# A recommender tower on one core: one first load, one batch of transposes in another PSUM bank, filler matmuls, every row gather held behind TensorE, and a small GpSimd write behind each gather of the last two tiles

## The reference, cut to what matters

```
e = stack([tbl_f[ids[:, f]] for f in range(26)], axis=1)      # 512 x 26 x 128
sd = einsum('bfd,bd->bf', e, dense)
ss = einsum('bfd,bgd->bfg', e, e);  pairs = ss[:, iu, ju]     # triu, k=1
z = concatenate([dense, sd, pairs], axis=1)
h = concatenate([z, dense], axis=1)                            # 607 columns
h = maximum(h @ W_top1 + b_top1, 0)                            # 512
h = maximum(h @ W_top2 + b_top2, 0)                            # 256
y = h @ W_top3                                                 # 1
```

## Time and profile before

| | us |
|---|---|
| median of 3 runs | 152.84 |
| the profiled execution's own time | 151.2 |
| its span, first to last instruction | 149.4 |
| TensorE busy | 108.6 |
| VectorE busy | 79.9 |
| ScalarE busy | 66.7 |
| GpSimd busy | 66.0 |

### The profile page before, as it was taken

One profiled execution on the slowest core, in us unless ns is written; L12 is line 12 of the kernel. 1 busy time (PEld: TensorE's weight loads), 2 busy tenths in 40 slices (PEclk: granted clock), 3 DMA queues, 4 the chain that ended last, 5 costly groups with the idle time before them and its releaser, 6 DMA issues.

```text
span 149.4 us, 2760 instructions
## 1 busy us (share of the span) xinstructions
PE 108.6 (73%) x1074; PEld 95.6 (64%) x1074; DVE 79.9 (53%) x217; ACT 66.7 (45%) x151; POOL 66.0 (44%) x66
## 2 busy tenths in 40 slices
PE   7799961999999925500001957958997999799794
PEld 7588831888888805400001947948986998699782
DVE  5699919979999274000750020680386189248401
ACT  4463309737786053000502041693398288145620
POOL 7787747768787778777783752000000000000000
PEclk9999996599999996855555699996999999999999
DMA  4877961576999422111120211000000000000000
GB/s 116 257 193 188 247 191 36 175 183 199 305 287 249 153 53 53 53 53 53 35 52 19 57 35 42 2 0 4 4 0 0 4 0 0 4 4 0 0 0 1
DMA packets 5030, 12.35 MB, mean 83 GB/s; under 512 B 1725, under 2 KB 1853, under 8 KB 5018
## 3 DMA queue, kind: packets, MB, share of 16 engines
q1 hardware_dynamic: 3002, 8.09, 18.8%
q0 software_dynamic: 1920, 3.94, 10.3%
q10 hardware_dynamic: 96, 0.15, 0.4%
HBM read 12.18 MB, written 0.00 MB: 82 GB/s over the span
## 4 chain that ended last, share of the span: by engine, by line
PE 47%; issue 16%; DVE 14%; another core or an unknown queue 13%; ACT 9%; ACTq 0%
PE dots L443 19%; DVE pairs L347 12%; PE dots L487 12%; PE hidden L512 4%; PE hidden L542 3%; PE turned L467 3%; ACT embT L310 2%; ACT high L299 2%; PE dots L421 2%; ACT embT L285 2%; ACT pairs L285 2%; PE turned L512 1%; DVE embT L347 1%; PE last_layers L535 1%
## 5 line engine op out<-in xcount | busy, mean ns | idle before, releaser
L249 POOL DMA_INDIRECT rows<-tbl,gather_idx x60 | 63.3, 1055 | 24.2 <-issue 16.5
L354 DVE TENSOR_SCALAR onehot<-ids_h 125x512 fp32r<-125x512 f16 x88 | 33.4, 435 | 22.5 <-issue 13.9
L443 PE MATMUL dots<-onehot,high 125*128 125x512 f32 (+1 forms) x88 | 36.0, 426 | 0.0
L347 DVE COPY pairs<-dots 27x128 f32<-27x128 f32 (+8 forms) x88 | 23.7, 270 | 21.7 <-PE dots L487 19.1
L467 PE MATMUL turned<-ident,rows 128*128 128x128 f32 x60 | 10.8, 305 | 31.7 <-ACT embT L285 21.5
L443 PE MATMUL dots<-onehot,low 125*128 125x512 f32 (+1 forms) x88 | 32.9, 389 | 0.3 <-issue 0.3
L467 PEld LDWEIGHTS turned<-ident,rows 128*128 128x128 f32 x60 | 7.6, 154 | 34.8 <-issue 34.1
L285 ACT COPY pairs<-dots 27x128 f32<-27x128 f32 (+8 forms) x88 | 20.9, 237 | 18.6 <-PE dots L487 16.6
L299 ACT CAST high<-table 125x1024 fp32r<-125x1024 f32 (+1 forms) x12 | 11.6, 979 | 34.8 <-issue 14.3
L443 PEld LDWEIGHTS dots<-onehot,high 125*128 125x128 f32 x88 | 19.0, 216 | 3.1
L487 PE MATMUL dots<-embT 128*64 128x54 f32 x512 | 17.6, 234 | 3.7 <-DVE pairs L347 2.0
(11 more groups left out here) (43 smaller groups left out, 74.2 us busy)
## 6 DMA issues: line engine op xcount, KB each, us to landing
table<-tbl SPq DMA_DIRECT2D x10, 448.0 KB
wp<-w_pairs SPq DMA_DIRECT2D x2, 512.0 KB
rows<-tbl,gather_idx POOLq DMA_INDIRECT x60
table<-tbl SPq DMA_DIRECT2D x10, 52.0 KB
wd<-w_dense SPq DMA_DIRECT2D x1, 512.0 KB
w2s<-w SPq DMA_DIRECT2D x1, 512.0 KB
table<-tbl SPq DMA_DIRECT2D x2, 224.0 KB
denseT<-dense_t SPq DMA_DIRECT2D x1, 256.0 KB
```

The lines of the kernel that those rows point to most:

```text
L249: pool.indirect_dma_start(out=rows[:, t % 2, n, :], out_offset=None, in_=tables[GATHERED_TABLES[n]][:, :], in_offset=bass.IndirectOffsetOn ...
L347: return nc.vector.tensor_copy(dst, src)
L354: nc.vector.tensor_scalar(onehot[:, i % 2, c, :], ids_h[:, i, :], float(c), None, ALU.is_equal).then_inc(onehot_ready, 1)
L443: last = nc.tensor.matmul(selected[t % 2][:, samples], part[:, t % 2, c, :], onehot[:, t % 2, c, samples], start=(part is high and c == 0) ...
```

## The change

- **Order of the steps.** B2.2 moves ahead of D1, B2.3 ahead of L0.0, B3.0 ahead of M0, B3.1 ahead of L1.0, B3.3 ahead of Y1, and Y0 ahead of D2. A new step W14 runs 14 filler matmuls after P1, once the second half of table 9 has been placed. The placers of batches 9 to 13 change.
- **Another bank.** Batch 10 (B2.2) is transposed into `last_layers`, not `turned`, so it needs not wait for batch 9 to be placed.
- **First load.** Ids and spreading matrix come in one DMA of 32 partitions, into the tile `first`; the spreading matrix is a view of it.
- **Memset of `pairs`.** VectorE does it in the last table's step and not at the start.
- **Gathers.** `GATHERS_AHEAD` is 6 and not 7. The hold by `table_selected` goes on for k up to 41. k = 42 and 46 also wait for D0, k = 51 and 54 for D1, and k = 57 for the first layer of tile 0 (both halves, L0.0 and L0.1). The waits for `transposed` stay.
- **Zeros.** Behind each of the 30 gathers of tiles 2 and 3, GpSimd writes 192 float32 zeros on each of 128 partitions to a tile `pace` that nobody reads. From the second on, each memset waits for the memset before it.

```
@@ sizes
+SPREAD_WORDS = len(ONEHOT_TABLES) * ROW_PARTS // 2 + 1
-    GATHERS_AHEAD, GATHERS_PER_TABLE = 7, 3
+    GATHERS_AHEAD, GATHERS_PER_TABLE = 6, 3
+    LATER_GATHERS = GATHERS_AHEAD + GATHERS_PER_TABLE * (N_ONEHOT + 1)
+    HELD_BY_DOTS, HELD_BY_LAYER1 = {42: 1, 46: 1, 51: 2, 54: 2}, {57: 2}
@@ tiles
+        pace = sb("pace", [128, 192])
-        ids_i = sb("ids_i", [ID_ROWS, BATCH], I32)
+        first = sb("first", [128, BATCH + SPREAD_WORDS], I32)
+        ids_i = first[0:ID_ROWS, 0:BATCH]
-        spread_f = sb("spread_f", [128, N_ONEHOT, ROW_PARTS], F16)
+        spread_f = first[:, BATCH:BATCH + SPREAD_WORDS].bitcast(F16)
@@ order
-            T10.0 B2.0 T9.3 T9.4 D0 C0.0 T10.1 T10.2 T10.3 T10.4 C0.1 P0 B2.1 P1
-            D1 C1.0 B2.2 L0.0 L0.1 R0 C1.1 B2.3 M0
-            B3.0 D2 C2.0 Y0 B3.1 L1.0 L1.1 R1 C2.1 P2 B3.2 M1
-            B3.3 D3 C3.0 Y1 L2.0 L2.1 R2 C3.1 P3 M2
+            T10.0 B2.0 T9.3 T9.4 D0 C0.0 T10.1 T10.2 T10.3 T10.4 C0.1 P0 B2.1 P1 W14 B2.2
+            D1 C1.0 B2.3 L0.0 L0.1 R0 C1.1 B3.0 M0 Y0
+            D2 C2.0 B3.1 L1.0 L1.1 R1 C2.1 P2 B3.2 M1 B3.3 Y1
+            D3 C3.0 L2.0 L2.1 R2 C3.1 P3 M2
-        PLACERS = [0, 0, 0, 0, 0, 0, 0, 0, 1, 0, 0, 1, 0, 0, 1, 1]
+        PLACERS = [0, 0, 0, 0, 0, 0, 0, 0, 1, 0, 1, 0, 1, 0, 1, 1]
+        APART = 2 * BATCHES + 2
@@ GpSimd
-                    behind = (t * N_GATHERED + n - GATHERS_AHEAD) // GATHERS_PER_TABLE
-                    if t < 2 and behind > 0:
-                        pool.wait_ge(table_selected, behind)
+                    k = t * N_GATHERED + n
+                    if GATHERS_AHEAD + GATHERS_PER_TABLE <= k < LATER_GATHERS:
+                        pool.wait_ge(table_selected, (k - GATHERS_AHEAD) // GATHERS_PER_TABLE)
+                    if k in HELD_BY_DOTS:
+                        pool.wait_ge(dots_done, HELD_BY_DOTS[k])
+                    if k in HELD_BY_LAYER1:
+                        pool.wait_ge(layer1_done, HELD_BY_LAYER1[k])
...
+                    if t >= 2:
+                        if k > 2 * N_GATHERED:
+                            pool.wait_ge(paced, k - 2 * N_GATHERED)
+                        nc.gpsimd.memset(pace[:, :], 0.0).then_inc(paced, 1)
@@ ScalarE
-            act.dma_start(spread_f[0:ID_ROWS, :, :], spread).then_inc(spread_loaded, 16)
-            act.dma_start(ids_i[:, :], onehot_ids).then_inc(onehot_ids_loaded, 16)
+            act.dma_start(first[0:ID_ROWS, :], first_needed).then_inc(first_needed_loaded, 16)
@@ VectorE
+                        nc.vector.memset(pairs[0:32, :, :, :], 1.0).then_inc(pairs_filled, 1)
...
-            nc.vector.memset(pairs[0:32, :, :, :], 1.0).then_inc(pairs_filled, 1)
@@ TensorE
+                if kind == "warming":
+                    pe.wait_ge(table_placed, N_ONEHOT + 1)
+                    warm(t)
...
+                    if n == APART:
+                        pe.wait_ge(table_placed, N_ONEHOT + 1)
+                    elif n >= 1:
+                        previous = n - 2 if n == APART + 1 else n - 1
+                        placer = batch_placer(previous)
+                        pe.wait_ge(batch_placed[placer], placed_by(placer, previous + 1))
...
                     if t == 0:
-                        pe.wait_ge(table_placed, N_ONEHOT + 1)
+                        placer = batch_placer(APART)
+                        pe.wait_ge(batch_placed[placer], placed_by(placer, APART + 1))
```

More of the change, by code:

```diff
@@ L44, with dlrm_tower @@
 PAIR_COPIES += [(3, 0, 12, 1, 4, 16), (2, 0, 3, 1, 4, 8), (0, 0, 0, 2, 2, 3)]
-def dlrm_tower(nc, gather_ids, onehot_ids, spread, tables, dense_t, w_pairs, w_dense, small, w2, identity,
+def dlrm_tower(nc, gather_ids, first_needed, tables, dense_t, w_pairs, w_dense, small, w2, identity,
                out):
@@ L152, in dlrm_tower @@
         y_ready = sem("y_ready")
+        paced = sem("paced")
         stored = sem("stored")
@@ L235, in _ @@
         def _(pool):
-            for first, last in ((ID_ROWS, 64), (64, 128)):
-                nc.gpsimd.memset(spread_f[first:last, :, :], 0.0).then_inc(spread_padded, 1)
+            for start, end in ((ID_ROWS, 64), (64, 128)):
+                nc.gpsimd.memset(spread_f[start:end, :], 0.0).then_inc(spread_padded, 1)
             pool.wait_ge(gather_ids_loaded, 16)
@@ L252, in _, with transposes_of @@
                     ).then_inc(gathered[t % 2][b], 16)
+                    if t >= 2:
+                        if k > 2 * N_GATHERED:
+                            pool.wait_ge(paced, k - 2 * N_GATHERED)
+                        nc.gpsimd.memset(pace[:, :], 0.0).then_inc(paced, 1)
+        def transposes_of(n):
+            return last_layers[:, :].rearrange("p (a b) -> p a b", a=BATCH_T) if n == APART else turned
         def place_batch(eng, copy, engine, t, b):
@@ L257, in place_batch @@
             copy(embT[:, t * TILE:(t + 1) * TILE, s:s + n].rearrange("p b s -> p s b"),
-                 turned[:, 0:n, :]).then_inc(batch_placed[engine], 1)
+                 transposes_of(batch_no(t, b))[:, 0:n, :]).then_inc(batch_placed[engine], 1)
         COPIES = [[(j, copy) for j in quarters for copy in PAIR_COPIES[0:4]] +
@@ L420, in spread_ids, with warm @@
                     pe.wait_ge(ids_relative, i - 1)
-                nc.tensor.matmul(relative[i % 2][0:ROW_PARTS, :], spread_f[:, i, :], ids_f[:, :], start=True, stop=True
+                nc.tensor.matmul(relative[i % 2][0:ROW_PARTS, :], spread_f[:, ROW_PARTS * i:ROW_PARTS * (i + 1)],
+                                 ids_f[:, :], start=True, stop=True
                                  ).then_inc(ids_spread, 1)
+            def warm(count):
+                for _ in range(count):
+                    nc.tensor.matmul(last_layers[:, 0:128], zeros[:, :], zeros[:, :], start=True, stop=True)
             def step(kind, t, i=0):
-                if kind == "table" and i == 0:
+                if kind == "warming":
+                    pe.wait_ge(table_placed, N_ONEHOT + 1)
+                    warm(t)
+                elif kind == "table" and i == 0:
                     if t + IDS_AHEAD < N_ONEHOT:
@@ L462, in step @@
                     pe.wait_ge(gathered[t % 2][i], 16 * BATCH_SIZE[i] * (t // 2 + 1))
-                    if n >= 1:
-                        placer = batch_placer(n - 1)
-                        pe.wait_ge(batch_placed[placer], placed_by(placer, n))
+                    if n == APART:
[4 more added lines that the diff above has]
+                        pe.wait_ge(batch_placed[placer], placed_by(placer, previous + 1))
                     for m in range(BATCH_SIZE[i]):
-                        last = nc.tensor.transpose(turned[:, m, :], rows[:, t % 2, BATCH_T * i + m, :],
+                        last = nc.tensor.transpose(transposes_of(n)[:, m, :], rows[:, t % 2, BATCH_T * i + m, :],
                                                    ident[:, :])
@@ L539, in _ @@
             pe.wait_ge(zeros_ready, 1)
-            def warm(count):
-                for _ in range(count):
-                    nc.tensor.matmul(hidden[0][:, 0, :], zeros[:, :], zeros[:, :], start=True, stop=True)
             warm(WARMING)
@@ L611 @@
     out = nc.dram_tensor("out", (1, BATCH), mybir.dt.float32, kind="ExternalOutput").ap()
-    dlrm_tower(nc, aps["gather_ids"], aps["onehot_ids"], aps["spread"],
-               [aps[f"tbl_{f}"] for f in range(FEATURES)], aps["dense_t"], aps["w_pairs"], aps["w_dense"],
+    dlrm_tower(nc, aps["gather_ids"], aps["first_needed"], [aps[f"tbl_{f}"] for f in range(FEATURES)], aps["dense_t"], aps["w_pairs"], aps["w_dense"],
                aps["small"], aps["w2"], aps["identity"], out)
```

22 lines of the change are left out of this document (10 added, 12 removed).

## The result

The change makes the kernel faster on this chip, by much less than forecast: 142.14 us, the median of four runs (140.62 to 142.58), against 151.88 us of the kernel before in the same job (149.25 to 153.49). The ratio is 0.9453 [0.9301, 0.9604]. The forecast was 123. The profiled execution took 142.37 us, its span is 140.6. In five later jobs, on chips that their records number 14, 0, 10, 3 and 11, the kernel before took 112.6 to 114.0 us (medians) and the change brought nothing; the record of the result has no number for its chip. The ratios leave out executions that took over 1.5% longer than the fastest of the same kernel, those of 125 to 129 us of the later jobs among them.

What follows compares the result with a forecast made beforehand. TensorE's signals, late beside unstopped gathers, were taken as the bound; without that hole (32.0 us) GpSimd bounds. D3 at 100.4 plus 20.8 gives span 121.2, with 1.8 around it 123 us; range 117 to 147.

Steps and rivals of the forecast that it cites:

- case (b): Rival: TensorE's late signals return in part, three (D0, D1, B2.3) some 4 us late each: 135, 128 to 147; chance 0.30.
- case (a): TensorE's signals prompt, GpSimd the bound: 123, from 117 to 128, or 139 at 2.18 us a gather; chance 0.52.
- GpSimd's count: Gathers of tiles 2 and 3 end at 96.6, so D3 starts at 100.4; the products' own sequence gives 96.5.
- chain of tiles: Products and VectorE's copies from D0's end at 62.6: D1 at 69.3, D2 at 83.0, D3 at 96.5.
- The start: Up to table 7: first load 0.6 us, one gather less ahead 1.2 us; together 1.8, table 7 at 46.8.
- the hold of k = 12: k = 12, not 13, first waits for table 1; GpSimd's run and the signal end 1.25 us earlier: 1.2 gained.
- The tables without the hole: After table 7, VectorE's one-hots of tables 9 and 10 end at 55.8; D0 ends at 62.6, before 94.63: 32.0 us gained.
- The products beside gathers: D0 from 58.5 to 62.6; D1 took 5.49 us before, and fillers may gain up to 1.5.
- The price of the zeros: Behind gathers of tiles 2 and 3: 192 zeros cost some 0.26 us; a gather takes 1.72 beside table work, later 1.58.
- GpSimd becomes the bound: Gathers k = 30 to 41 end at 68.1, k = 42 to 59 at 96.6; D3 starts at 100.4.
- Rival (c): Slower: zeros don't help signals, each waits for a gather run's end plus 1.9 us: 153, or 157; chance 0.14.
- The reading behind it all: While GpSimd issues gathers unstopped, TensorE's signals come late (4.4, 18.3, 21.8, 23.8 us); they come through when it stops.

Runs made afterwards that it cites:

- e6_after_again: The changed kernel, unedited, run again beside the kernel before on chip 0: 114.99 us, 1.0112 of the kernel before.
- e5_before_again: The kernel before, unedited, run again on chip 0: 113.52 us (one run, span 111.7).
- e14_holds_alone_paired: The kernel before with the new holds alone, no zeros, on chip 3: 112.98 us, 0.9981 of the kernel before.

## Why the prediction was wrong

The direction was right, the size wasn't: 9.7 us came off the median where some 29 had been forecast. The step that failed is the cost of TensorE's own work and signals beside gathers, which the sum put at nothing: D0 at 4.1 us and D1 at 5.5, and no wait for a signal behind them. The run showed 9.35 and 10.92 us, and 6.1 us more between D1 and D2. What happened is case (b), late signals that come back in part, with 0.30 (135, 128 to 147), and not case (a), with 0.52. The terms, against the forecast span of 121.2:

| | forecast | measured | difference |
|---|---|---|---|
| table 7's end | 46.8 | 47.07 | +0.3 |
| D0 starts | 58.5 | 63.63 | +5.1 |
| D0 takes | 4.1 | 9.35 | +5.3 |
| D0's end to D1's start | 6.7 | 6.77 | 0 |
| D1 takes | 5.5 | 10.92 | +5.4 |
| D1's end to D2's start | 8.2 | 14.33 | +6.1 |
| D2 takes | 3.94 | 5.98 | +2.0 |
| D2's end to D3's start | 9.6 | 9.31 | -0.3 |
| GpSimd's count, by which D3 was put later than the chain of tiles | 3.9 | 0 | -3.9 |
| from D3's start to the end | 20.8 | 20.3 | -0.5 |

The first row is inside the second; the others add to the 19.4 us by which the span is longer than forecast.

**The start** held in its size: 1.55 us by table 7 (48.62 to 47.07) where 1.8 was forecast. The one load gave 0.94 (the cast at 3.83 in place of 4.77) where 0.6 was taken, the hold of k = 12 gave less: VectorE went on at 21.61 and not at 22.35. The step took the run to end 1.25 us earlier by one gather. It ended 0.5 earlier (20.05 against 20.58), since the first gather started at 4.27 and not at 3.57, and the signal followed by 1.6 us where it had been 1.8: the mechanism held.

**The tables without the hole.** This step failed in part. It let the signals of tables 8 and 9 come at once. Table 8's came 2.8 us late, with k = 31 and 32 streaming beside it, and TensorE stood 3.55 us before B1.3 (57.42) for what hung on it; behind that its granted clock was 0.72 until 63.6. Together: 5.1 us by D0's start. Before it was 18 us and more, so most of the hole did go.

**The products beside gathers.** This is the step that failed, and with D0 (5.3 us), D1 (5.4) and the signals behind D1 (6.1) it is most of the 19.4. The prediction took D0 at 4.1 and D1 at 5.49 from the trace of before, where no gather ran beside them but for one: D0 there stood 0.85 us on "issue" in the middle, 0.98 us behind the start of gather k = 59. That row was in the timeline, and it had a term that the change multiplies: by the prediction's own count gathers would run all along D0 and D1. At one pause of 0.85 us in each period of 1.58, products of 3.94 us take 8.5; measured were 9.35 and 10.92. That the clock would fall as well isn't in that row; D1's 5.49 us, with no gather near and a granted clock of 0.69, had that price on it. D2 shows it after the change: 5.98 us at 0.62, behind 5.2 us in which TensorE was busy for 0.4.

**Rival (b)** named three late signals of 4 us. None of the three was on the path: VectorE's copies start 0.04 us behind D0 and 0.03 behind D1, when GpSimd stands at its hold. Late on the path were table 8's signal, and behind D1 that of layer 1 (2.1 us), that of batch B3.0 (done by 95.3, taken up at 98.26 by a VectorE that was free from 97.30) and those of layer 2. So the mechanism of (b) held, its places didn't, and 135 came nearer to the time for partly other reasons.

**The price of the zeros** held: 0.27 us a memset, 0.40 to 0.45 beside VectorE's table work, 0.30 on average, against 0.26. **GpSimd becomes the bound** failed: behind a memset the next gather starts 0.17 us later and not 0.30, and with no table work beside it a gather takes 0.95 and not 1.02. The period there is 1.39, not 1.58; beside table work it was 1.68 on average (k = 30 to 35), near the 1.72. GpSimd idled 4.5 and 5.3 us at its holds for D0 and D1. That k = 41 was done at 68.75, where 68.1 had been forecast, is luck: k = 30 started at 50.75 and not at 47.5, and the gathers made up for it. Gathers beside VectorE's copies of products took 0.95 us (from 73.25 on), those beside the one-hots 0.94 to 1.46 and one 3.65 (k = 16, from 27.83). The rule of the Trainium skill that the prediction weighed (SBUF — State Buffer, Who interferes with whom) has the trace on its side for the copies.

**Rival (c)**, slower, didn't happen on the chip of the result, and its rule (a signal waits for the end of a run plus 1.9 us) is too strong for the tables and for D0. On the other chips the change is 1.010 and 1.011, by another mechanism than (c).

**The reading behind it all** was that gathers cause the lateness. What the runs leave of it: in both traces of that chip no signal is late once the last gather has ended, and the pauses keep the gathers' period of 1.4 us; the same gathers, in the same kernel, cause none in the five later jobs. But a dense stream isn't enough even on that chip, and the prediction's own trace had this in it. Before the change GpSimd issued 34 gathers, k = 19 to 52, from 32.37 to 78.64 with 0.30 us between them, not only the 25 from 45.21 on, and the signals of tables 4, 5 and 6 came through that stream within 0.1 us. Table 5, in the timelines of TensorE, ScalarE and GpSimd before:

```profile
40.21 0.39 PE L443 MATMUL dots<-onehot,low 125*128 125x512 f32 x1
...
40.70 1.05 ACT L299 CAST high<-table 125x1024 fp32r<-125x1024 f32 x1 [0.96 <-PE dots L443]
...
39.39 1.35 POOL L249 DMA_INDIRECT rows<-tbl,gather_idx  x1 [0.30 <-issue]
41.05 1.09 POOL L249 DMA_INDIRECT rows<-tbl,gather_idx  x1 [0.31 <-issue]
```

So "three gathers per table" didn't describe that stretch, and the holds can't be what kept its signals prompt. Gathers go with the lateness, something of that chip or that job is a condition, and there is a third thing that tells 32 to 45 us from 49 to 79. Neither was found. Whether what reaches TensorE late is a signal, an instruction or something else wasn't tried, and neither was whether the holds, the zeros or the new order brought the 9.7 us, since no later job met this behaviour. The rule in rival (c), from the Trainium skill (VectorE: DVE Perf Modes, The TRN2 errata), is stronger there than the prediction put it: frequent increments from one engine can deadlock another. No run here stood still, and e6_after_again, with 30 increments more, has no late signal; for the chip of the result it is untested.

## What to carry to other kernels

A hole in which an engine's work is done and nobody is told need not belong to the kernel: run the kernel before in another job, on another chip, before you tune against it, since here the gap between jobs (152 to 113 us) was four times the gain. Before a reading becomes a rule, look in the same trace for a stretch where its condition holds and its effect doesn't: 32 to 45 us was one. And where a trace shows an interference at one place, price it at every place to which the change moves the same pair of engines, the producer's own instructions included and not only its signals. Look for its smallest instance in rows that seem harmless: the one gather beside D0 in the trace of before had the price on it.

## What the runs showed of the hardware

- One kernel takes 149 to 153 us in one job and 112.6 to 114.0 (medians) in five others on five chips. Of the 37.7 us between the spans of before and e5_before_again, 6.5 have come up by table 7's end, 36.2 by D0's end, and the rest is D1 at its lower clock (5.49 against 3.94). They lie in TensorE's late signals (up to 23.8 us) and in the lower clock around them: D3 takes 3.94 us in both.
- In the result's run TensorE did 4 or 5 small matmuls per gather of GpSimd in the paused parts of D0 and D1, where alone it does some 45 in the same 1.39 us (128 in 3.94 us).
- A memset of 192 float32 on 128 partitions takes 0.27 us on GpSimd (0.40 to 0.45 beside VectorE's one-hots), one of 576 0.59, one of 1024 0.95, and one of 192 or 576 put between two gathers shortens the gap ahead of the next from 0.30 to 0.17 us.
- Executions of 125 to 129 us came in all five later jobs, in the kernel before in four of them. The six that were profiled have one gather that keeps GpSimd for 11.4 us (k = 14, in the two with the new first load) or 15.3 us (k = 15, in the four with the old one), from 23.5 to 24.2 us on, and TensorE waits 11.6 to 13.0 us for rows. The 3.65 us of k = 16 in the result's run, at 27.83, may be a small case of it. In the timeline of GpSimd of e14_holds_alone_paired:

```profile
23.85 15.27 POOL L256 DMA_INDIRECT rows<-tbl,gather_idx  x1 [0.30 <-issue]
```
